# Reordering the opening of a one-core Perceiver block: loads, first projections and late weights

## What is computed

```python
x = x + xattn(layernorm(x), ctx, ctx, mask)   # 16 heads of 32; ctx: 32 batches x 257 rows x 512
x = x + linear_attn(layernorm(x))             # elu(q)+1, elu(k)+1, causal sums, Wout, layernorm
x = x + moe(layernorm(x))                     # shared expert, 64 experts of width 256, top 8 of each token
```

## Time and profile before

| | |
|---|---|
| median of three runs | 1462.96 us |
| the profiled execution, its own time | 1465.62 us |
| its span, first to last instruction | 1463.8 us |
| mean granted TensorE clock | 0.963 of 2.4 GHz |
| busy share: TensorE, weight loads, VectorE, ScalarE, GpSimd | 91%, 70%, 53%, 43%, 28% |
| DMA, mean over the span | 139 GB/s |

### The profile page before, as it was taken

One profiled execution on the slowest core, in us unless ns is written; L12 is line 12 of the kernel. 1 busy time (PEld: TensorE's weight loads), 2 busy tenths in 40 slices (PEclk: granted clock), 3 DMA queues, 4 the chain that ended last, 5 costly groups with the idle time before them and its releaser, 6 DMA issues. The chain is left out here.

```text
span 1463.8 us, 26879 instructions
## 1 busy us (share of the span) xinstructions
PE 1339.3 (91%) x7106; PEld 1031.6 (70%) x7107; DVE 780.7 (53%) x1813; ACT 628.1 (43%) x1310; POOL 404.5 (28%) x322
## 2 busy tenths in 40 slices
PE   4999999999999999999998795499999999999991
PEld 3888787888887888788885542367667776676670
DVE  3445566565655665655554344465655565656550
ACT  1444343343343333443432113266656556656550
POOL 0000030030030200300301102455665465766441
PEclk8999999999999999999998898699999999999996
DMA  8321110111110101101003002599999999999985
GB/s 317 133 96 32 31 46 16 45 31 38 37 31 30 45 15 44 31 29 39 24 1 101 30 21 109 193 290 301 339 300 317 284 319 318 351 300 306 284 222 86
DMA packets 66896, 204.19 MB, mean 139 GB/s; under 512 B 16015, under 2 KB 18319, under 8 KB 56480
## 3 DMA queue, kind: packets, MB, share of 16 engines
q1 hardware_dynamic: 42960, 159.19, 30.1%
q0 software_dynamic: 23888, 44.40, 14.3%
HBM read 176.73 MB, written 37.03 MB: 146 GB/s over the span
## 5 line engine op out<-in xcount | busy, mean ns | idle before, releaser
L1298 DVE TENSOR_TENSOR gul<-wgu,guh 128x2048 fp32r<-128x2048 f32 x71 | 162.9, 2294 | 74.9 <-ACT guh L1251 58.2
L372 POOL TENSOR_TENSOR rstd<-vep,half 128x1 f32<-128x1 f32 x32 | 17.7, 553 | 637.4 <-DVE vep L532 637.2
L1454 PE MATMUL ebank<-wd,ht 128*128 128x512 f32 x380 | 175.1, 593 | 1.0 <-ACT ht L1236 1.0
L453 ACT ACTIVATE kt<-bank,colb 128x256 f32<-128x256 f32 x128 | 60.4, 472 | 243.5 <-PE bank L823 243.3
L821 PE MATMUL bank<-ch,wkh 128*128 128x256 f32 x512 | 161.0, 314 | 1.4 <-issue 0.5
L1424 PE MATMUL ebank<-guh,xth 128*128 128x512 f32 x380 | 155.6, 409 | 4.0 <-DVE gul L1298 2.3
L1426 PE MATMUL ebank<-guh,xtl 128*128 128x512 f32 x380 | 149.2, 393 | 0.0
L1425 PE MATMUL ebank<-gul,xth 128*128 128x512 f32 x380 | 149.0, 392 | 0.0
L1176 POOL DMA_INDIRECT xg<-xn_rows,ig x95 | 127.6, 1344 | 75.6 <-issue 42.3
L823 PE MATMUL bank<-ch,wkl 128*128 128x256 f32 x512 | 144.7, 283 | 0.4 <-issue 0.4
L822 PE MATMUL bank<-cl,wkh 128*128 128x256 f32 x512 | 144.8, 283 | 0.0
(11 more groups left out here) (227 smaller groups left out, 2672.7 us busy)
## 6 DMA issues: line engine op xcount, KB each, us to landing
wgu<-in_egu SPq DMA_DIRECT2D x71, 1024.0 KB
wd<-in_edn SPq DMA_DIRECT2D x71, 512.0 KB
craw<-in_ctx SPq DMA_DIRECT2D x32, 514.0 KB, 3.2
wqkv<-in_wqkv SPq DMA_DIRECT2D x1, 3072.0 KB, 17.0
second_sums<-x1b SPq DMA_DIRECT2D x9, 256.0 KB, 3.8
xa<-in_x SPq DMA_DIRECT2D x8, 256.0 KB, 2.8
xr<-in_x SPq DMA_DIRECT2D x8, 256.0 KB, 3.5
xn_rows<-xn SPq DMA_DIRECT2D x8, 256.0 KB, 2.1
```

The source lines that it names most:

```text
L1298: V.tensor_tensor(gul[par][:, :, :], wgu[w][:, :, :], guh[par][:, :, :].bitcast(F32), ALU.subtract).then_inc(s_w["gu_low"], 1)
L1454: last = mm(y_ps[tile.half][:, :], tile.ht[:, c, :], wd[item.w][:, c, :], start=c == 0, stop=c == IC - 1)
```

## The change

Five edits, all in stage A:

1. SyncE asks for wq behind the context of batch 0 instead of ahead of wk. The seven later weights are asked for in pass 0 at b = 1, k = 2 (that is, in the second batch), instead of before the zeros.
2. ScalarE runs a 1x1 exponential (`warm`) as its first instruction, copies `xat` ahead of `high(0, 0)`, and does `q_blocks(0, 0)` at b = 0, k = 3 instead of before the batches.
3. VectorE handles only batch 0's last row before `low(0, 0)`; batch 1's comes after the split of wv, and `pre_q(0)` (its `qt`) behind that. `vlc` and the clearing of `qz` move to b = 1, k = 3.
4. TensorE starts batch 0 as soon as wk is split. The queries' matmuls (`pre_q(0)`) and the wait for the split wv stand ahead of the values at b = 0, k = 4; the last rows' values are made at the end of b = 0, k = 5; the wait for `vlc` is at b = 2, k = 0.
5. A new 1x1 tile, `warm_a`.

```diff
-            sp.dma_start(wq[:, :, :], d.wq).then_inc(s_wq, 16)
             sp.dma_start(raw[:, :, :], d.wk).then_inc(s_wk, 16)
...
             load_ctx(0, 0, True)
+            sp.dma_start(wq[:, :, :], d.wq).then_inc(s_wq, 16)
             load_ctx(0, 1, True)
...
-            for dst, src in ((wo, d.wo), (rowb, d.rowb), (wqkv, d.wqkv), (wout, d.wout), (gate, d.gate), (sgu, d.sgu), (sdn, d.sdn)):
-                sp.dma_start(dst[:, :, :], src).then_inc(s_wrest, 16)
...
                 if k == 1 and front and (nxt or b < 2):
                     load_ctx(t, b + 2)
+                if k == 2 and b == 1 and type(t) is int and t == 0:
+                    for dst, src in ((wo, d.wo), (rowb, d.rowb), (wqkv, d.wqkv), (wout, d.wout), (gate, d.gate), (sgu, d.sgu), (sdn, d.sdn)):
+                        sp.dma_start(dst[:, :, :], src).then_inc(s_wrest, 16)
...
         def _(act):
+            act.wait_ge(s_pad, 1)
+            nc.scalar.activation(warm[:, :], half[0:1, :], ACT.Exp)
             act.wait_ge(s_cn, 32)
...
-            high(0, 0)
             act.wait_ge(s_pt, 1)
             nc.scalar.copy(xat[:, :, :], sc_ps[0][:, :].rearrange("p (c n) -> p c n", c=DC)).then_inc(s_pte, 1)
-
+            high(0, 0)
             act.wait_ge(s_pad, 4)
-            q_blocks(0, 0)
...
                 if k == 3 and front:
+                    if b == 0 and type(t) is int and t == 0:
+                        q_blocks(0, 0)
                     if b < 3:
                         q_blocks(t, b + 1)
...
             negate_last(0, 0)
-            negate_last(0, 1)
             dve.drain()
             low(0, 0)
             masks(0, 0)
-            pre_q(0)
             dve.wait_ge(s_wv, 16)
             V.tensor_copy(wvh[:, :, :], raw[:, :, :])
             dve.drain()
             V.tensor_tensor(wvl[:, :, :], raw[:, :, :], wvh[:, :, :].bitcast(F32), ALU.subtract).then_inc(s_wvd, 1)
-            dve.wait_ge(s_vlps, 1)
-            V.tensor_tensor(vlc[:, :, :], px[0][:, 0:DC * NB].rearrange("p (c n) -> p c n", c=DC),
-                            colb[:, 2, :].unsqueeze(2).to_broadcast([P, DC, NB]), ALU.add).then_inc(s_vlsb, 1)
-            V.memset(qz[:, :, :, :], 0.0)
+            negate_last(0, 1)
+            pre_q(0)
...
+                if k == 3 and b == 1 and type(t) is int and t == 0:
+                    dve.wait_ge(s_vlps, 1)
+                    V.tensor_tensor(vlc[:, :, :], px[0][:, 0:DC * NB].rearrange("p (c n) -> p c n", c=DC),
+                                    colb[:, 2, :].unsqueeze(2).to_broadcast([P, DC, NB]), ALU.add).then_inc(s_vlsb, 1)
+                    V.memset(qz[:, :, :, :], 0.0)
+                    dve.drain()
...
             pre_t(0)
-            pe.wait_ge(s_wq, 16)
-            pre_q(0)
-
-            pe.wait_ge(s_ctl, 16)
-            pe.wait_ge(s_wvd, 1)
-            for g in range(DC):
-                for c in range(DC):
-                    last = mm(px[0][:, g * NB:(g + 1) * NB], raw[:, c, g * P:(g + 1) * P], ctl[:, c, :], start=c == 0, stop=c == DC - 1)
-            last.then_inc(s_vlps, 1)
-            pe.wait_ge(s_vlsb, 1)
             pe.wait_ge(s_wkd, 1)
+
+            def last_values():
+                pe.wait_ge(s_ctl, 16)
+                for g in range(DC):
+                    for c in range(DC):
+                        last = mm(px[0][:, g * NB:(g + 1) * NB], raw[:, c, g * P:(g + 1) * P], ctl[:, c, :], start=c == 0, stop=c == DC - 1)
+                last.then_inc(s_vlps, 1)
...
+                if b == 0 and k == 4 and type(t) is int and t == 0:
+                    pe.wait_ge(s_wq, 16)
+                    pre_q(0)
+                    pe.wait_ge(s_wvd, 1)
+                if b == 2 and k == 0 and type(t) is int and t == 0:
+                    pe.wait_ge(s_vlsb, 1)
                 if k >= 4 and front:
...
+                if k == 5 and b == 0 and type(t) is int and t == 0:
+                    last_values()
```

More of the change, by code:

```diff
@@ L130, in stage_a @@
         cap = [sb(f"cap{i}", [P, S]) for i in range(2)]
+        warm = sb("warm_a", [1, 1])
         kt = sb("kt", [P, DC, S])
```

## The result

| | before | changed |
|---|---|---|
| median of seven runs on one chip | 1462.09 us | 1452.80 us |
| lowest and highest | 1459.90, 1463.28 | 1445.57, 1457.14 |
| profiled execution, its span | 1465.62, 1463.8 | 1457.14, 1455.4 |

The ratio is 0.9939, with a 95% interval of 0.9916 to 0.9962: faster by 0.6%. The forecast was 1450.4, range 1446.0 to 1455.5; the medians lie 9.3 us apart where 12.6 had been forecast. The profiled execution is the slowest of the seven, so the traces are compared stage by stage, not by their ends.

A forecast was written before the change was run, and what follows sets the result against it. TensorE is 91% busy, so time lies in the opening, where keys wait on program order: 21.0 - 0.5 - 3.5 - 0.8 - 3.6 = 12.6 us gained, from median 1462.96 to 1450.4 us; range 1446.0 to 1455.5.

The forecast's parts named there:

- keys of batch 0: First 48 matmuls of batch 0: 8.3 us, with 5.6 us of it at 1.2 GHz, costing 0.5 us.
- new wait before score matmul 3: TensorE in batch 0: score copies come later because q blocks wait for the queries; stall 0.65 to 1.1, taken as 0.8 us.
- The start: Opening: batch 0's keys start at 15.1 instead of 36.07, 21.0 us earlier, with wk's cast at 7.9.
- Rival B: Opening: another load or step is last, batch 0 starts or runs 2 to 5 us later; 1452 to 1456 us, chance 0.10.
- The rest of batch 0: Batch 0 behind keys and queries: 7.14 us as today, besides the 0.8 us stall and 3.6 us of last values.
- The table load: ScalarE's opening: 1.28 us load moves to idle time at `warm`; without that cover it would cost 1.3 us again.
- The weights: SyncE: seven weights (8.1 MB) asked for at about 34, in by about 56; craw(1,0) behind them has 8 us of cover.
- rival D: Moved weights hold up craw(1,0), VectorE stands at nl in batch 2; slower, 1466 us, chance 0.03.
- the cover of 3.5 us: Batch 0: wv lands 19.8 at the latest, its split ends 23.4, queries end 26.9; 3.5 us to spare.
- head start of VectorE: Batch 1: last values give VectorE 3.6 us, taken as larger cover for its moved steps; without cover these cost 2.1 us.
- Rival A: Clock falls during the 32-column last values, slowing the keys behind them; 1453 to 1456 us, chance 0.12.
- Rival C: Gain given back later by another clock phase or a wait at the second stage's handover; 1460 to 1465 us, chance 0.05.

The follow-up runs named there:

- changed_again: The changed kernel again, its second-stage waits on loaded values masked with one more register operation; median 1454.3 us against 1466.45 for the kernel before, ratio 0.9922.
- weights_early: Against the changed kernel (waits masked): the seven later weights asked for ahead of the zero rows again; 1469.98 us, one run.
- no_warm: Against the changed kernel (waits masked): without ScalarE's first activation, the `warm` exponential; 1455.47 us, one run.
- idle_fill_32: Against the changed kernel (waits masked): 14 unread fp32 matmuls of 32 columns in TensorE's idle time before the first keys; 1452.51 us, one run.
- idle_fill_128: Against the changed kernel (waits masked): 14 unread fp32 matmuls of 128 columns in TensorE's idle time before the first keys; 1450.14 us, one run.
- three first runs: Three runs of the kernel before, cited in the prediction; median 1462.96 us, within 1.2 us of each other.

## Why the prediction was right

The mechanism was right: the keys of batch 0 waited on the order of TensorE's program, and what was moved behind them came back at the price that had been summed. In size the time of the whole kernel was further off than the stage, 9.3 us on the first chip and 12.2 on the second against 12.6. By the prediction's own steps:

| step | forecast | changed | changed_again |
|---|---|---|---|
| cast of wk starts | 7.9 | 8.76 | 8.30 |
| first keys | 15.1 | 16.03 | 15.56 |
| keys of batch 0 | 8.3 us | 8.25 | 8.30 |
| queries | 3.5 us | 3.49 | 3.48 |
| new wait before score matmul 3 | 0.8 us | 0.74 | 0.74 |
| rest of batch 0 without that wait and the values | 7.14 us | 7.68 | 7.68 |
| last rows' values | 3.6 us | 3.49 | 3.49 |
| batch 1 | 38.4 | 39.68 | 39.25 |
| gain at that point and at matmul 200 | 12.6 | 11.3, 12.2 | 11.7, 12.5 |

That the gain at matmul 200 meets the 12.6 is in part luck: batch 1 came 0.9 to 1.3 us late, and 0.8 us that were not in the sum came back inside it. So is the 8.3 us of the keys: the clock rose 5.6 us after their start, as taken, but in other traces with the same opening of TensorE's program the first stretch of the keys at the lower clock lasted anything from 3.2 us (weights_early) to 5.8 us (no_warm).

**The start** came 0.5 to 0.9 us late. The row from which wk's landing was read, wq's 5.7 us in the old place, was too short: in the same place wk took 6.6 and 6.1 us. The old norm's end, 7.61, was 8.24 in the first trace and 7.62 in changed_again; the cast stood behind wk in both. The rest of the chain ran as summed, 16.03 - 8.76 = 7.27 us from cast to keys where 7.2 had been worked out. Rival B was this miss in kind, not in size.

**The rest of batch 0** took 0.5 us more than the 7.14 that were read off the old trace, at the first value matmul and around the new wait; a smaller stall and shorter last values gave 0.2 back.

**The table load** was mis-argued. "Without that cover it would cost 1.3 again" is refuted by no_warm: the earlier copy of xat is cover enough. The sum wasn't touched by it. The drain that the Trainium skill, page "ScalarE: Activation LUTs", section "What ACT_TABLE_LOAD costs", adds to the load doesn't show in the changed kernel either: the load ends at 2.05 and its activation starts at 2.07. For these loads the trace decides. ScalarE was idle ahead of the load in the traces of the kernel before, the changed one and no_warm; what a load right behind other work costs, no run shows.

**The weights.** Their move cost nothing visible: nl in batch 2 (66.94) follows `low` without a wait, so rival D didn't come. The cover was thinner than the stated 8 us: they were asked for from 35.6 on, the last landed at 61.5 instead of about 56, and craw(1,0), asked for at 50.65, landed 10.5 us later, at 61.2. wv was "19.8 at the latest" and landed at 20.4; the cover of 3.5 us was in truth 3.75, because everything behind it was late too. That the old place of the weights would have become a stall was right, and weights_early gave its size, 15.87 us on VectorE, which I had not put into a number.

**Batch 1** gave 0.84 us (0.8 also in changed_again). I had counted the head start of VectorE as cover alone. It also brings the exponentials forward, which had held up the copies of the keys: in the kernel before TensorE waits for such a copy inside batch 1, in the changed kernel it doesn't, and there 0.7 of the 0.84 us arise.

```profile
56.05 0.39 PE L821 MATMUL bank<-ch,wkh 128*128 128x256 f32 x1 [0.45 <-ACT kt L453]
```

**Rival A**, a fall of the clock in the last values, didn't occur in any trace with the values in batch 0 (in weights_early it had fallen before them, in the wait). In idle_fill_32 the clock stayed at the lower level through 6.02 us of such matmuls; that it would fall from the upper one in them doesn't follow.

**Rival C** took its part. The gain of 12.2 us at matmul 200 is 8.4 at 7000: 1.2 are lost in the passes and 3.5 between 4500 and 7000, 0.9 come back between. Over fourteen traces that last stretch took 648.1 to 654.0 us, whatever the opening was; the changed kernel's first trace has the highest of all, changed_again 649.6. The two parts that vary are the end of stage A, which took 139.7 to 143.6 us (matmul 4500 to 5000), and the experts, and they vary with the falls of the granted clock: the last stretch had 78.5 us at 1.2 GHz in the changed kernel's first trace, 71.7 in the kernel before and 68.3 in changed_again. Half of the 6.8 us between the first two is 3.4, about what was lost. So the 9.3 us of the first chip and the 12.2 of the second are the same change under different falls, as far as these traces tell. That the three first runs lay within 1.2 us was no argument: eleven runs of the kernel before on another chip reach from 1456.72 to 1470.47.

## What to carry to other kernels

Ask of every step ahead of the main loop whether the loop needs it, and move what it doesn't need behind the first iteration; a step that costs 7 us at the lower clock and waits for its own load cost 3.5 us there. Before a step is moved forward, look for the wait that will be late next: here it was the completion of a small store behind 8 MB of loads, and in weights_early it turned the gain into a loss. Where an engine with a granted clock must idle before its main work, fill that time, best with real work, and look in the trace whether the level rose: here it did behind one filler and not behind the other.

## What the runs showed of the hardware

- TensorE, busy without a gap on 32-column fp32 matmuls from a start at 1.2 GHz, stayed there for 6.02 us in idle_fill_32 and for 7.00 us in the kernel before; in idle_fill_128, on as many matmuls of 128 columns as in idle_fill_32, it came up to 2.4 GHz within their 4.86 us.
- A store of 256 KB landed 21.0 us (before) and 20.6 us (weights_early) after its ask with 8 MB of loads asked for ahead of it on the same queue, and 4.7 us after it without them.
- The row of granted clock reads 1.00 from the start of the span (17 to 20 us in the kernel before), while the queries' matmuls there last up to 551 ns, as at the lower clock. For the opening, before the first recorded change, the durations are to be believed.
- A wait of 14.10 us cost TensorE a further 3.2 us in the last values alone, 6.87 us against 3.65.
- Single executions of one kernel spread over up to 14 us (1456.72 to 1470.47 for the kernel before, 1445.57 to 1457.14 for the changed one), and in the seven runs of the changed kernel the spread goes with the granted clock, while batch 1 starts within 2.4 us in three traces at the old opening and within 0.5 us in two at the changed one: for a gain of 12 us in one stage the trace of that stage is the better measure.
